# A fused two-layer network on one core: the last batch's gates, mixing sums and joins regrouped, with a second buffer for the last pair

## The reference

```python
wv = _topk_mask(gl_v, SEL) * jax.nn.sigmoid(gl_v)       # b t h e
xv = jnp.einsum('btd,edk->btek', x, Wv)
v = jnp.einsum('bthe,btek->bhtk', wv, xv)               # values mixed
...
attn = jnp.einsum('bhij,bhjd->bihd', probs, v)
mask_o = _topk_mask(gl_o, SEL)
out = jnp.einsum('bthe,bthk,ekd->btd', mask_o, attn, Wo)  # outputs gated
```

## Time and profile before

| | us |
|---|---|
| median of 3 runs | 2792.52 |
| lowest, highest | 2789.43, 2797.73 |
| the profiled execution | 2793.39 |
| its span, first to last instruction | 2791.7 |
| PE, DVE, ACT, POOL busy in it | 2336.8, 1882.4, 1695.5, 1862.2 |

### The profile page before, as it was taken

The page is one execution under the profiler, slowest core; times in us unless marked ns, Lnnn a source line. Parts: engine busy times, 40 slices in busy tenths (PEclk is TensorE's granted clock), DMA queues, the critical chain, the costliest instruction groups (busy, mean ns, idle before and its releaser), DMA issues. The chain is left out here.

```text
span 2791.7 us, 31646 instructions
## 1 busy us (share of the span) xinstructions
PE 2336.8 (84%) x10169; PEld 1176.0 (42%) x10169; DVE 1882.4 (67%) x3123; ACT 1695.5 (61%) x2439; POOL 1862.2 (67%) x1978
## 2 busy tenths in 40 slices
PE   5667778777777777785888899989999999999996
PEld 2222323232333323223555445545555555555543
DVE  5888989898888988764333356566666656566574
ACT  1778888979888888990122264545554545555445
POOL 0555577787878687874577302959595958677776
PEclk8668787878788787777899899999999999999998
DMA  3000000000000010115699500000000000000000
GB/s 105 16 1 1 18 16 16 18 15 19 8 19 15 10 23 3 24 17 112 192 272 242 121 1 1 1 1 16 8 16 9 16 8 16 8 9 1 1 8 16
DMA packets 94103, 98.98 MB, mean 35 GB/s; under 512 B 18897, under 2 KB 90705, under 8 KB 93905
## 3 DMA queue, kind: packets, MB, share of 16 engines
q1 hardware_dynamic: 70752, 73.99, 9.2%
q0 software_dynamic: 23152, 22.68, 4.6%
HBM read 69.98 MB, written 26.66 MB: 35 GB/s over the span
## 5 line engine op out<-in xcount | busy, mean ns | idle before, releaser
L1049 POOL TENSOR_TENSOR TT<-TT,SS 128x512 f32<-128x512 f32 x512 | 651.8, 1308 | 221.8 <-ACT SS L978 221.2
L1816 ACT ACTIVATE PR<-S,NM 128x512 f32<-128x512 f32 x512 | 344.8, 685 | 263.5 <-DVE NM L2000 263.5
L2000 DVE TENSOR_REDUCE NM<-S 128x2 f32<-128x1024 f32 x256 | 301.6, 1219 | 134.0 <-PE S L1706 134.0
L734 DVE TENSOR_SCALAR TT<-SC 128x1024 f32<-128x1024 f32 x256 | 311.4, 1216 | 72.7 <-POOL TT L1049 44.6
L464 PE MATMUL OB<-TT,VAL 128*17 128x512 f32 x1024 | 343.6, 774 | 4.8 <-ACT TT L986 4.8
L736 DVE SCALAR_TENSOR_TENSOR SS<-SC,TT 128x1024 f32<-128x1024 f32 x256 | 313.5, 1225 | 20.6 <-issue 1.8
L1054 POOL DMA_INDIRECT slot_tokens<-TID,IDX x224 | 229.0, 1022 | 101.1 <-issue 67.1
L1717 PE MATMUL TP<-ident,PR 128*128 128x128 f32 x2048 | 272.9, 276 | 19.9 <-DVE TT L2005 15.4
L1717 PEld LDWEIGHTS TP<-ident,PR 128*128 128x128 f32 x2048 | 235.9, 142 | 109.9 <-issue 69.3
L2005 DVE COPY TT<-TP 128x512 f32<-128x512 f32 x256 | 176.1, 688 | 143.4 <-PE TP L1717 139.6
L1822 ACT ACTIVATE TT<-TP 128x512 f32<-128x512 f32 x256 | 153.1, 598 | 177.3 <-PE TP L1717 173.4
(11 more groups left out here) (296 smaller groups left out, 4084.1 us busy)
## 6 DMA issues: line engine op xcount, KB each, us to landing
TT<-w_gu SPq DMA_DIRECT2D x64, 384.0 KB
TT<-w_dn SPq DMA_DIRECT2D x64, 128.0 KB
XL<-x SPq DMA_DIRECT2D x8, 512.0 KB
stream<-V SPq DMA_DIRECT2D x4, 1024.0 KB, 10.4
rows<-XL SPq DMA_DIRECT2D x8, 512.0 KB
TT<-w_dn SPq DMA_DIRECT2D x64, 64.0 KB
XS<-stream SPq DMA_DIRECT2D x8, 512.0 KB, 4.5
X<-x SPq DMA_DIRECT2D x7, 512.0 KB
```

Of the source, the lines that this page charges most:

```text
L734: dve.tensor_scalar(tt[:, :, mt, :], SC[mt % 2][:], 0.0, None, ALU.max)
L1049: ins = pool.tensor_tensor(tt, tt, ss, ALU.add)
L1816: act.activation(PR[s % 2][h2][:], S[s % 2][:, h2, :], ACT.Exp, bias=NM[:, s % 2, h2:h2 + 1], accum_out=SM[:, pair % 2, j, h2:h2 + 1]).the ...
L2000: dve.tensor_reduce(NM[:, s % 2, :], S[s % 2][:], AX, ALU.max, negate=True).then_inc(sems["peak"], 1)
```

## The change

`sum_own` is cut into halves of two token tiles, eight instead of four. Those of pairs 0 and 1 stay where the whole was, those of pair 2 go to Z and D3 of d=3, and the weighing and both halves of pair 3 go to d=6 and d=7. ACT's first four `own_gate` halves go from D3 of d=4, 5, 6, 7 to Z of d=5, 6, 7, 7. `own_gate` of pair 3 writes VW and waits for that pair's mixing sum (`vh_own`) in place of the second addition; `own_sum` of pair 3 reads VW, and every `own_sum` gets a drain in front. In the tail's table all four joins stand first, which changes DVE's order alone.

```diff
@@ PREP_2_LAST
-    (1, 1, A, "weigh_own", 0), (1, 1, D3, "sum_own", 0), (1, 2, A, "weigh_own", 1), (1, 2, Z, "sum_own", 1),
-    (1, 2, D3, "weigh_own", 2), (1, 3, D3, "sum_own", 2), (1, 4, D3, "weigh_own", 3), (1, 5, D3, "sum_own", 3))
+    (1, 1, A, "weigh_own", 0), (1, 1, D3, "sum_own", 0), (1, 1, D3, "sum_own", 1),
+    (1, 2, A, "weigh_own", 1), (1, 2, Z, "sum_own", 2), (1, 2, Z, "sum_own", 3),
+    (1, 2, D3, "weigh_own", 2), (1, 3, Z, "sum_own", 4), (1, 3, D3, "sum_own", 5),
+    (1, 6, D3, "weigh_own", 3), (1, 7, Z, "sum_own", 6), (1, 7, Z, "sum_own", 7))
@@ OUT_2_TAIL
-OUT_2_TAIL = table((0, 4, 4, "join", 0), (0, 4, 4, "turn_last", 0), (0, 4, 4, "join", 1), (0, 4, 4, "turn_last", 1),
-                   (0, 4, 4, "product_last", 0), (0, 4, 4, "join", 2), (0, 4, 4, "turn_last", 2), (0, 4, 4, "product_last", 1),
-                   (0, 4, 4, "join", 3), (0, 4, 4, "turn_last", 3), (0, 4, 4, "product_last", 2), (0, 4, 4, "product_last", 3))
+OUT_2_TAIL = table((0, 4, 4, "join", 0), (0, 4, 4, "join", 1), (0, 4, 4, "join", 2), (0, 4, 4, "join", 3),
+                   (0, 4, 4, "turn_last", 0), (0, 4, 4, "turn_last", 1), (0, 4, 4, "product_last", 0), (0, 4, 4, "turn_last", 2),
+                   (0, 4, 4, "product_last", 1), (0, 4, 4, "turn_last", 3), (0, 4, 4, "product_last", 2), (0, 4, 4, "product_last", 3))
@@ HEADS_2_TAIL
-    (0, 4, D3, "own_gate", 0), (0, 5, D3, "own_gate", 1), (0, 6, D3, "own_gate", 2), (0, 7, D3, "own_gate", 3),
+    (0, 5, Z, "own_gate", 0), (0, 6, Z, "own_gate", 1), (0, 7, Z, "own_gate", 2), (0, 7, Z, "own_gate", 3),
@@ ACT own_gate
-                    if pair >= 2:
-                        act.wait_ge(sems["own"], pair - 1)
-                dst = (GT_OWN if pair else GL_OWN).rearrange("p j (e d) -> p j e d", e=SE)
+                    if pair == 2:
+                        act.wait_ge(sems["own"], 1)
+                    if pair == 3:
+                        act.wait_ge(sems["vh_own"], PAIRS1)
+                dst = VW[:] if pair == 3 else (GT_OWN if pair else GL_OWN).rearrange("p j (e d) -> p j e d", e=SE)
@@ DVE own_sum
-                dve.tensor_tensor(GL_OWN, GL_OWN, GT_OWN, ALU.add).then_inc(sems["own"], 1)
+                add = VW[:].rearrange("p j e d -> p j (e d)") if pair == 3 else GT_OWN
+                dve.drain()
+                dve.tensor_tensor(GL_OWN, GL_OWN, add, ALU.add).then_inc(sems["own"], 1)
@@ DVE sum_own
-            def sum_own(v, pair, b):
-                h = 2 * pair + 1
-                dve.drain()
-                dve.tensor_reduce(VN[set_for(2, b)][:, :, h * DH1:(h + 1) * DH1], VW[:].rearrange("p j e d -> p j d e"),
-                                  AX, ALU.add).then_inc(sems["vh_own"], 1)
+            def sum_own(v, i, b):
+                pair, h = i // 2, i - i % 2 + 1
+                at = slice(NT // 2 * (i % 2), NT // 2 * (i % 2) + NT // 2)
+                if i % 2 == 0:
+                    dve.drain()
+                ins = dve.tensor_reduce(VN[set_for(2, b)][:, at, h * DH1:(h + 1) * DH1], VW[:, at].rearrange("p j e d -> p j d e"),
+                                        AX, ALU.add)
+                if i % 2:
+                    ins.then_inc(sems["vh_own"], 1)
```

## The result

The changed kernel took 2780.19 us (median of 8 runs, 2776.32 to 2785.95) against 2792.68 us (8 runs, 2789.43 to 2802.82) of the kernel before: ratio 0.995, 95% interval 0.9937 to 0.9963. I had forecast 2784.4 us, a gain of 8.1 us, and so put the larger chance, 0.50, on no measurable change. The median lies within the range, but the whole interval lies beyond the 0.3%: it is a measurable gain, and that forecast was wrong.

What follows compares the result with a forecast made beforehand. Bound: when the join can begin, set after the change by GpSimd, ending at 2775.67 - 3.95 + 1.15 = 2772.9. With the tail, 8.1 us off: 2793.39 profiled becomes 2785.3, less 0.9 to the median, 2784.4 us; range 2780.0 to 2788.5.

Steps and rivals of the forecast that it cites:

- case A: Tail: GpSimd sets the end and joins take turns with it; 8.1 us gained, chance 0.57.
- The PE path: Last run's double steps d=0 to d=7 on TensorE: heads of pairs 2 and 3 divided 8.2 us earlier, unknown between 3 and 9.
- The new wait at d=6: Double step 6 of the last run: TensorE stands 1.6 us because pair 2's attention needs GpSimd's fourth mixing group.
- rival D: TensorE's clock falls to 1.2 GHz after new idle time and stays: about 10 us slower, 2802, chance 0.05.
- the gates: At d=4 ACT's ten gatings delay its copy, TensorE waiting 1.43 us more; moved, this goes, with 0.9 us lost at d=5.
- The second buffer: Pair 3's gating on ACT no longer waits for DVE's second addition: 3.9 us off, last addition over near 2765.3.
- The wait: GpSimd's 3.95 us wait for the heads of pair 2, claimed to go whole.
- the collisions: DVE's 1280-element additions lengthen GpSimd's work by 1.04 to 1.24 us each; a seventh adds 1.15 us.
- The 4.8 us that I gave the other thread in hand: Lead of the ACT and DVE thread over GpSimd's first tile of its last sum, forecast at 2770.4.
- The splitting of the sums: DVE's mixing sums in halves: four more instructions cost some 0.1 us each, bounds 0 and 0.2 us.
- Joins first: Tail: joins run beside GpSimd's additions, about 1.0 us each; addition and join (0.9 us) go twice between product and next transposes.
- the 8.4 us bound: About 0.3% of the kernel's time, what a measurement can tell from no change.

Runs made afterwards that it cites:

- a_act_twice: Changed kernel with ACT gating tiles 2 and 3 of pair 3's even head a second time: 91.5 us from GpSimd's mixing start to the last addition's end, ratio 0.9961.
- a_novw: Changed kernel without the second buffer VW (old own_gate and own_sum): 90.1 us from GpSimd's mixing start to the last addition's end, ratio 0.9953.
- a_share: Changed kernel with two tiles of the last odd head gated by ACT and added by DVE instead of GpSimd: 89.5 us from GpSimd's mixing start, ratio 0.9949.
- a_again: Changed kernel run again with nothing edited: 91.4 us from GpSimd's mixing start to the last addition's end, ratio 0.9955.
- a_oldgates: Changed kernel with ACT's first four gated halves back behind the numerators (d=4 to d=7): 95.5 us from GpSimd's mixing start, ratio 0.9973.
- a_oldsums: Changed kernel with DVE's sums of pair 2 and weighing and sums of pair 3 back in their old steps: 91.5 us from GpSimd's mixing start, ratio 0.9966.
- a_warm: Changed kernel with 20 unused filling matmuls on TensorE before the first join: 95.5 us from GpSimd's mixing start, ratio 0.9983.

## Why the prediction was right and where it was wrong

**What bounds the kernel.** Right: GpSimd was close behind the thread over ACT and DVE, and after the change it sets the join (a_act_twice, a_novw, a_share). It was case A.

**The PE path.** I gave 8.2 us; pair 2's heads came 8.9 us earlier, pair 3's 8.1, and in a_again 7.3 and 7.0. The new wait at d=6 (1.6 us forecast) was 0.54 us here and 2.18 in a_again, where pair 1's heads came 1.7 us sooner. Behind the 2.18 us the attention took 3.19 us for 1.94, at a granted clock of 0.58 (2739.5 to 2743.6), and 1.00 again from 2743.6: the start of rival D, which ended by itself and was covered by GpSimd. For the gates I had named the right copies but not their worth: without their move the heads come 9.5 us later (a_oldgates), more than the whole gain.

**The second buffer.** The last addition was over at t = 74.6, forecast 2765.3 - 2690.95 = 74.4. Its 3.9 us are all covered: a_novw lost nothing. As step of the sum that was right, since I counted only GpSimd's wait.

**GpSimd.** Its end came at t = 83.0; I had 2772.9 - 2690.95 = 82.0. The wait gave 3.8 us, the collisions cost 0.45 us more than I took (the six before lengthened GpSimd's groups by 7.1 us together, the seven after by 8.7), and the joins delayed it by another 0.5 us, which I had left out. The first join came 0.7 us later than forecast. The 4.8 us that I gave the other thread in hand are 5.1 by my own times (2770.4 - 2765.3); DVE's wait was 5.54 us here and 3.71 in a_again.

**The splitting of the sums.** Two halves took 2.44 to 2.48 us for 2.35 to 2.42: 0.1 us, as costed. The Trainium skill's advice for the fewest instructions (VectorE: DVE Perf Modes, Rules for kernel authors) holds by that amount, and whether it is covered was not tried by itself; the places of the sums did not matter (a_oldsums).

**Joins first: here the sum failed.** The step says that the chain before has, twice, 0.9 us between a product and the next transposes, and that this goes: 1.8 us. It left out that the clock goes with it: the traces show the order of the joins together with how long TensorE stays at 1.2 GHz. And I took one profiled execution's tail, 12.0 us, as the kernel's; two further traces have 15.5 and 15.6. From the first join's start to the end I had forecast 11.05 us for 12.0, a gain of 0.9; the means of three traces each are 14.4 before and 11.6 after, a gain of 2.7. The part up to the first join was right in size: 7.0 us, for 7.15 forecast. The mean stretch before is (98.6 + 102.8 + 102.8) / 3 = 101.4 us, after (91.9 + 91.4 + 91.9) / 3 = 91.7: 9.7 us, for 8.1 forecast and 6.7 in the first pair. That is over the 8.4 us bound, so the likelier outcome should have been faster. The first pair of traces alone would not have shown it. I had rival D for a clock that falls after the change, but none for a clock that had cost the kernel before more than its one trace showed.

**The rest.** 9.7 us in the stretch stand against 12.5 (10.3 to 17.6 by the interval), 12.6 (9.2 to 16.2) and 8.7 us (5.0 to 12.6) in the three comparisons of times. What lies between is within what three traces and the wandering start of GpSimd leave open; that a part is gained ahead of the stretch isn't shown by any run: over all twenty traces GpSimd's mean start is later, not earlier, in those made from the changed kernel. That the median came out at 2780.19, inside the range of 2780.0 to 2788.5, is in part luck, since the sum gives no reason for the last 2.8 us.

## What to carry to other kernels

Before costing a tail from one profile, look at the clock in it: products behind a long wait of TensorE can take twice their time (here 2.77 us for 1.46), and how many do differs from run to run of one kernel, so that a chain read in one execution may be several us short (here 3.5). Put what feeds TensorE (here, four joins) in front of what only drains it. And when a thread is shortened, count the next engine's whole list from its start: here GpSimd's fixed list gave its new end within 1.1 us, while the second buffer, taken back by itself, turned out to be covered by it, and the new places of the sums turned out to bring nothing.

## What I had not expected of the hardware

- The same program's tail took 12.0, 15.5 and 15.6 us, with granted clocks of 0.57 rising to 1.00 in one and 0.50 over twelve us in another. All three have stops of 0.92 us between products; without the stops, three traces of the changed kernel took 11.6 to 11.7 us.
- A DVE addition of 1280 elements lengthens whatever GpSimd does by 1.0 to 1.3 us, and two in one group by 2.5 us (5.86 for 3.3); joins of 320 elements beside GpSimd's additions of the same size take 0.9 us each for 0.5 and cost GpSimd 0.5 us over three of them.
- A float32 matmul of 128 x 128 by 512 columns appears as two instructions and takes 0.87 us (a_warm, 17.33 us for twenty).
